# GpSimd makes three of eight query-key products, VectorE reads its queries from PSUM, and the orders around them are rewritten

## The chip, the cores and the metric

The kernel runs on one core of a Trainium2 chip. The metric is the device time of one execution in microseconds; lower is better. The kernel before takes 84.03 us, the median of three runs (83.32 to 84.17).

## The reference, cut to what matters

Two layers with residuals on x of 8 images, 128 channels, 16 x 16 positions, all in float32. The first is a dilated 3 x 3 neighbourhood attention whose four channel groups of 32 (two heads of 16 each) have dilations 1, 2, 4 and 8; each group's output is scaled by a gate, a softmax over pooled features. The second is a channel attention with projections. Each layer normalises its input over groups of four channels.

```python
def L0(x, w_qkv, w_gate, b_gate):            # x is group-normalised
    qkv = einsum('bchw,oc->bohw', x, w_qkv).reshape(B, 3, 4, 32, H, W)
    for i, dil in enumerate((1, 2, 4, 8)):
        q, k, v = qkv[:, 0, i], qkv[:, 1, i], qkv[:, 2, i]
        # per head, per position: 9 neighbours at distance dil, zero outside
        attn = softmax(einsum('bhdn,bhdkn->bhnk', q, unfold3x3(k)) * 16 ** -0.5)
        outs[i] = einsum('bhnk,bhdkn->bnhd', attn, unfold3x3(v))
    gate = softmax(x.mean(axis=(2, 3)) @ w_gate.T + b_gate)
    return concatenate([outs[i] * gate[:, i] for i in range(4)])

def L1(x, W, b, W_proj, b_proj):             # x is group-normalised
    p = (einsum('oc,bchw->bohw', W, x) + b).reshape(B, 4, 32, 256)
    att = softmax(einsum('bhdn,bhen->bhde', p, p) * 256 ** -0.5)
    return einsum('oc,bchw->bohw', W_proj, einsum('bhde,bhen->bhdn', att, p)) + b_proj

x = x + L0(gn(x));  x = x + L1(gn(x))
```

## The kernel before

Every engine has an order written out by hand, and semaphores tie the orders together. The first layer works in two phases `ph` (even and odd images), and within a phase in four units `s`, one for each dilation; a unit (ph, s) holds 32 channels of four images on 128 partitions. The stages are:

- **Loads.** SyncE and ScalarE issue the loads of x in six pieces (`load_x`). SyncE loads the matrix that averages over a channel group (`C_GRP` of `cs`) between the first and the second of its pieces.
- **First norm.** VectorE sums, ScalarE sums squares, TensorE averages over groups (`first_stats`, L817), VectorE makes the variance (`norm_variance`, L536), GpSimd the power -0.5 (`rsqrt`, L334), then VectorE and ScalarE normalise. TensorE runs dummy matmuls between (`keep_clock`, L812) on the first slot of `xt`.
- **Projections.** `project` (L828) makes a tile of queries, keys or values in PSUM and ScalarE copies it out (`copy_tile`, L405), 21 tiles in five banks. Three units' queries, (0,0), (1,2) and (1,3), stay in PSUM (`project_query`, L847).
- **Products.** VectorE multiplies queries by shifted keys (`multiply_qk`, L582), three chunks a unit. TensorE sums them over channels of a head into scores (`sum_scores`, L864).
- **Softmax.** VectorE shifts (`softmax_shift`), ScalarE takes the exponential, VectorE divides (`softmax_divide`, L611) and multiplies in the gate, which GpSimd works out from L354 on. The result is `prob`.
- **Values.** TensorE spreads `prob` over channels (`spread`, L890), three chunks a unit, in two PSUM places by turns; VectorE multiplies by shifted values (`multiply_pv`, L621); the nine neighbours are added, eight additions a unit, by GpSimd for units (0,0) to (0,3), (1,0) and (1,1) (L374), and by VectorE for (1,2) (`add_neighbours`, L641). For (1,3) TensorE adds them up itself (`sum_second`, L924).
- **Back to images.** `restore(0)` and `restore(1)` (L911) put phase 0 back into image layout after GpSimd's 32nd addition; `sum_second` does so for phase 1. VectorE adds the residual (`first_residual`), ScalarE squares, TensorE averages (`group_stats`), VectorE makes the variance (`second_variance`), GpSimd the power (placed among its additions by `RSQRT_AFTER`), VectorE the bias (`second_norm_bias`, `nbias`), and ScalarE normalises (`norm`, L435).
- **Second layer**, in four groups of two images: projection, transposes, channel attention, softmax, fused projection, last residual, stores. TensorE's order has `attention(1)` of the second group just ahead of `sum_second`, so phase 1 of the first layer isn't put back before phase 0's attention is made.

Of the kernel before, what the change touches and what calls it, by code (L numbers as in the profile page):

```python
# [31 lines left out]
ARRIVAL = (0, 2, 6, 4, 1, 3, 5, 7)  # L32
NORMS_ON_DVE = ((2, 0), (3, 0), (3, 1))
# [7 lines left out]
RSQRT_AFTER = ((1, 0, 4), (1, 1, 0))  # L41
# [10 lines left out]
C_ID, C_GRP, C_RED, C_DIL, C_END = 0, 128, 256, 384, 388  # L52
# [52 lines left out]
def build(nc, x, wpack, consts, selc, out):  # L105
    with ExitStack() as ctx:
# [6 lines left out]
        xt = sb("xt", [P, B, N])  # L113
# [25 lines left out]
        warm = sb("warm", [P, 1])  # L139

# [31 lines left out]
        PROJ_BANKS = (0, 1, 2, 3, 6)  # L172
        IDLE_BANK = 5
        BANK = (4, 6, 0, 2)
        Q_IN_PSUM = [(0, 0, 0)] + [(0, s, PHASES - 1) for s in range(2, ND)]

        def q_columns(s):

            return 512 * SC[0] + N * (s % 2) if s else 512 * IDLE_BANK
# [6 lines left out]
        grp_loaded = sem("grp_loaded")  # L186
# [4 lines left out]
        cells_set = sem("cells_set")  # L191
        sum_ready = sem("sum_ready")
# [16 lines left out]
        qk_ready = sem("qk_ready")  # L209
        scores_ready = sem("scores_ready")  # L210
# [38 lines left out]
        tiles = []  # L249
        for ph in range(PHASES):  # L250
            tiles += [(kind, s, ph) for s in range(ND) for kind in (0, 1) if (kind, s, ph) not in Q_IN_PSUM]
            tiles += [(2, s, ph) for s in range(ND)]

        def x_slice(i):

            piece = X_PIECES[i]
            return slice(piece[0], piece[-1] + 1, PHASES)
# [26 lines left out]
        def _(sp):  # L284
            xv = x.rearrange("b c n -> c b n")

            def load_x(i):

                bs = x_slice(i)
                sp.dma_start(xt[:, bs, :], xv[:, bs, :]).then_inc(x_loaded[i], 16)  # L290
# [21 lines left out]
        def _(pool):  # L312
# [31 lines left out]

            pool.wait_ge(nbias_ready, PHASES)
# [16 lines left out]
            nc.gpsimd.tensor_tensor(gate[:], gsel[:], grec[:], ALU.mult).then_inc(gate_ready, 1)  # L362

# [19 lines left out]
        def _(act):  # L383
            xv = x.rearrange("b c n -> c b n")
            for i in (1, 3):
                bs = x_slice(i)
                act.dma_start(xt[:, bs, :], xv[:, bs, :]).then_inc(x_loaded[i], 16)
# [4 lines left out]
            def square_sum(n):  # L392
# [3 lines left out]
                nc.scalar.activation(xn1[:, b // GB, b % GB, :], xt[:, b, :], ACT.Square,  # L396
                                     accum_out=sums[:, b, 1:2]).then_inc(square_ready, 1)

            def first_norm(b):

                act.wait_ge(nbias_ready, b % PHASES + 1)
                nc.scalar.activation(xn[:, b, :], xt[:, b, :], ACT.Identity, bias=nbias[:, b:b + 1],
                                     scale=rstd[:, b:b + 1]).then_inc(xn_act_ready, 1)

            def copy_tile(n):  # L405
# [4 lines left out]
                act.wait_ge(proj_ready, n + 1)  # L410
                src = ps[:, PROJ_BANKS[n % len(PROJ_BANKS)], 0:N]
# [56 lines left out]
            for n in range(1, 3):  # L468
# [3 lines left out]
            copy_tile(3)  # L472
            copy_tile(4)
            copy_tile(5)
            first_norm(5)
            first_norm(7)
            for n in range(6, 12):
                copy_tile(n)
            gate_exp()
            for n in range(12, 17):  # L480
                copy_tile(n)
            softmax_exp(0)
            for n in range(17, len(tiles)):
                copy_tile(n)
            softmax_exp(1)
            squares(0)
# [33 lines left out]
        def _(dve):  # L520
# [7 lines left out]

            link(nc.vector.memset(signs[:, 0:1], -1.0))
# [31 lines left out]
            def channel_sum(n):  # L561
# [3 lines left out]
                nc.vector.tensor_reduce(sums[:, b, 0:1], xt[:, b, :], AX.X, ALU.add).then_inc(sum_ready, 1)  # L565

            def first_norm(b):
                dve.wait_ge(rstd_ready, b % PHASES + 1)
                nc.vector.tensor_scalar(xn[:, b, :], xt[:, b, :], gst[:, b, 0:1], rstd[:, b:b + 1],
# [12 lines left out]
            def multiply_qk(ph, s, ci):  # L582

                if ci == 0:
                    dve.wait_ge(proj_copied, tiles.index((1, s, ph)) + 1)
# [556 lines left out]
```

## Time and profile before

| | |
|---|---|
| median of three runs | 84.03 us (83.32 to 84.17) |
| the profiled execution | 84.19 us, of which the span of the trace is 82.3 us |
| TensorE matmul busy | 69.5 us (84%) |
| VectorE busy | 67.4 us (82%) |
| GpSimd busy | 41.5 us (50%) |
| ScalarE busy | 29.4 us (36%) |

All later times are counted from the start of the span. In the rows PE is TensorE, DVE VectorE, ACT ScalarE, POOL GpSimd, SP SyncE. A row of the timeline merges neighbouring instructions of one kind; a float32 matmul leaves two records, so x24 is 12 matmuls. A number in square brackets at a row's end is how long the engine sat idle before it, with the one that released it.

### The profile page before, as it was taken

Reading aid. Unit: us, or ns where it says so; the run is one execution under the profiler, and the core shown is the slowest. Engines: PE = TensorE matmul, PEld = TensorE weight load, DVE = VectorE, ACT = ScalarE, POOL = GpSimd, SP = SyncE. Lnnn points to the kernel's source line nnn. Section 1 sums busy time; section 2 is a strip of 40 time slices with the busy share of each in tenths; the row PEclk is TensorE's granted clock in tenths of the full one; section 3 lists DMA queues with packets and bytes.
Section 4 is the critical chain, followed back from the end, with each engine's and each line's share of the span. In section 5 each row is a group of like instructions: output and inputs, shape, how many; then the busy total and the mean of one; then the engine's idle time right before and its main releaser. Section 6 shows DMA issues by size and latency. Waiting matters only on the chain.

```text
span 82.3 us, 2430 instructions
## 1 busy us (share of the span) xinstructions
PE 69.5 (84%) x988; PEld 49.5 (60%) x988; DVE 67.4 (82%) x183; ACT 29.4 (36%) x92; POOL 41.5 (50%) x84
## 2 busy tenths in 40 slices
PE   0379999699995699899978879679999999999960
PEld 0369876266752359566768654368677768566530
DVE  1242869999999998999999699889999998587860
ACT  1852652992377000000020001240795362765210
POOL 7104105850770007999999999699992004200000
PEclk9999999999999999999999999999999999999999
DMA  0973046000000000000000000000000000002253
GB/s 4 284 223 127 0 92 158 15 0 0 8 0 4 0 4 8 0 0 0 4 8 0 0 0 0 0 0 8 0 0 0 8 0 8 4 33 94 79 176 127
DMA packets 3195, 3.04 MB, mean 37 GB/s; under 512 B 368, under 2 KB 3056, under 8 KB 3184
## 3 DMA queue, kind: packets, MB, share of 16 engines
q1 hardware_dynamic: 2896, 2.63, 11.5%
q10 hardware_dynamic: 288, 0.26, 0.9%
q8 instruction: 7, 0.11, 0.6%
q14 instruction: 4, 0.03, 0.1%
HBM read 1.84 MB, written 1.05 MB: 35 GB/s over the span
## 4 chain that ended last, share of the span: by engine, by line
DVE 50%; PE 28%; POOL 6%; issue 5%; DMA 5%; ACT 2%; SPq 1%; DVEq 0%
PE ps L810 26%; DVE qk L597 18%; DVE pv L638 12%; DMA xt<-x_dram 5%; POOL acc L374 3%; DVE acc L650 2%; DVE pv L650 2%; DVE x L669 2%; DVE prob L617 2%; DVE smax L604 2%; POOL rstd L337 2%; DVE ssum L614 2%; POOL pv L374 2%; DVE acc L638 1%; PE ps L967 1%
## 5 line engine op out<-in xcount | busy, mean ns | idle before, releaser
L810 PE MATMUL ps<-prob,sel 64*128 64x192 f32 (+6 forms) x192 | 17.8, 313 | 2.7 <-DVE pv L638 1.6
L810 PE MATMUL ps<-xn,wp 128*32 128x256 f32 (+1 forms) x208 | 18.0, 409 | 0.8 <-ACT q L413 0.7
L638 DVE TENSOR_TENSOR pv<-ps,v 128x128 f32<-128x128 f32 (+7 forms) x32 | 17.1, 567 | 1.8 <-PE ps L810 0.8
L810 PEld LDWEIGHTS ps<-prob,sel 64*128 64x128 f32 x192 | 13.6, 186 | 6.9 <-DVE pv L638 3.5
L810 PE MATMUL ps<-xt 128*128 128x128 f32 x60 | 11.7, 337 | 3.5 <-DMA xt<-x_dram 3.5
L374 POOL TENSOR_TENSOR pv<-pv 128x240 f32<-128x240 f32 (+3 forms) x24 | 14.1, 599 | 0.5 <-DVE pv L638 0.5
L337 POOL TENSOR_TENSOR rstd<-gvar,mhalf 128x2 f32<-128x2 f32 (+1 forms) x6 | 4.9, 809 | 17.0 <-DVE gvar L544 17.0
L810 PEld LDWEIGHTS ps<-xn,wp 128*32 128x32 f32 (+1 forms) x208 | 9.7, 122 | 5.9 <-ACT xn L439 1.3
L374 POOL TENSOR_TENSOR acc<-acc,pv 128x256 f32<-128x256 f32 (+4 forms) x20 | 12.7, 638 | 0.5
L810 PEld LDWEIGHTS ps<-xt 128*128 128x128 f32 x60 | 9.6, 232 | 4.8 <-DMA xt<-x_dram 3.5
L597 DVE TENSOR_TENSOR qk<-q,k 128x672 f32<-128x672 f32 (+7 forms) x21 | 11.4, 606 | 0.0
L810 PE MATMUL ps<-qk,cs 128*32 128x192 f32 (+6 forms) x176 | 7.7, 302 | 0.8 <-ACT v L416 0.8
L424 ACT ACTIVATE ps<-shifted 128x576 f32<-128x576 f32 x2 | 1.3, 655 | 16.7 <-DVE shifted L607 16.7
L597 DVE TENSOR_TENSOR qk<-ps,k 128x128 f32<-128x128 f32 (+6 forms) x15 | 6.4, 482 | 0.8 <-PE ps L810 0.8
L810 PEld LDWEIGHTS ps<-qk,cs 128*32 128x32 f32 x176 | 4.8, 109 | 3.5 <-ACT v L416 1.3
L432 ACT ACTIVATE pT<-x 128x256 f32<-128x256 f32 x8 | 3.3, 409 | 10.1 <-DVE x L669 10.1
L374 POOL TENSOR_TENSOR acc<-pv 128x256 f32<-128x256 f32 x4 | 2.9, 728 | 6.3 <-DVE pv L638 6.3
L565 DVE TENSOR_REDUCE sums<-xt 128x1 f32<-128x256 f32 x8 | 2.9, 413 | 3.1 <-DMA xt<-x_dram 3.1
L810 PE MATMUL ps<-p,mT 128*128 128x256 f32 x16 | 4.9, 410 | 0.3 <-ACT mT L459 0.3
L701 DVE SCALAR_TENSOR_TENSOR x<-ps,wp,x 128x256 f32<-128x256 f32 x8 | 3.7, 479 | 0.7 <-PE ps L810 0.7
L396 ACT ACTIVATE xn<-xt 128x256 f32<-128x256 f32 x8 | 3.3, 408 | 2.2 <-DMA xt<-x_dram 2.2
L439 ACT ACTIVATE xn<-x,nbias,rstd 128x256 f32<-128x256 f32 x5 | 2.7, 591 | 3.5 <-DVE nbias L550 3.5
(81 smaller groups left out, 89.6 us busy)
## 6 DMA issues: line engine op xcount, KB each, us to landing
out_dram<-x SPq DMA_DIRECT2D x8, 128.0 KB, 1.7
xt<-x_dram SPq DMA_DIRECT2D x2, 256.0 KB, 4.6
xt<-x_dram ACTq DMA_DIRECT2D x2, 128.0 KB, 2.9
xt<-x_dram SPq DMA_DIRECT2D x2, 128.0 KB, 3.2
sel<-selc_dram SPq DMA_DIRECT2D x4, 64.0 KB, 2.1
wp<-wpack_dram SPq DMA_DIRECT2D x1, 194.0 KB, 4.3
wp<-wpack_dram SPq DMA_DIRECT2D x1, 131.0 KB, 2.7
cs<-consts_dram SPq DMA_DIRECT2D x2, 64.0 KB, 2.6
```

The costliest lines, as they stand in the source:

```text
L337: nc.gpsimd.tensor_tensor(rstd[:, bs], gvar[:, bs], mhalf[:, bs], ALU.pow).then_inc(rstd_ready, 1)
L374: nc.gpsimd.tensor_tensor(o, a, b, ALU.add).then_inc(added, 1)
L396: nc.scalar.activation(xn1[:, b // GB, b % GB, :], xt[:, b, :], ACT.Square, accum_out=sums[:, b, 1:2]).then_inc(square_ready, 1)
L432: nc.scalar.activation(pT[:, g, 2 * i:2 * i + 2, :].rearrange("p t n -> p (t n)"), x1[:, b, :], ACT.Square, accum_out=sums1[:, b, 1:2]).th ...
L439: nc.scalar.activation(xn1[:, g, i, :], x1[:, b, :], ACT.Identity, bias=nbias[:, b:b + 1], scale=rstd[:, b:b + 1]).then_inc(xn1_act_ready, 1)
L565: nc.vector.tensor_reduce(sums[:, b, 0:1], xt[:, b, :], AX.X, ALU.add).then_inc(sum_ready, 1)
L597: last = nc.vector.tensor_tensor(o, a, b, ALU.mult)
L604: link(nc.vector.tensor_reduce(smax[:], view(ps, 512 * SC[ph], [[1, QP], [256, 3], [QP, 3]]), AX.XY, ALU.max))
L638: last = nc.vector.tensor_tensor(o, a, b, ALU.mult)
L650: nc.vector.tensor_tensor(o, a, b, ALU.add).then_inc(dve_added, 1)
L701: nc.vector.scalar_tensor_tensor(out=x1[:, b, :], in0=ps[:, BANK[g] + i, 0:N], scalar=wp[:, W_BP:W_BP + 1], in1=x1[:, b, :], op0=ALU.add, ...
L810: return nc.tensor.matmul(o, w, m, start=start, stop=stop)
```

## The change

- GpSimd makes the products of units (0,3), (1,2) and (1,3) (`multiply_qk` of its own, both operands in SBUF). The first two stand ahead of the gate's arithmetic, the third between the gate and the additions.
- VectorE makes the other five, all with the queries in PSUM (`Q_AT`); the order of its units in phase 0 is now 0, 2, 1.
- 19 tiles are copied by ScalarE instead of 21, from three banks, the six last value tiles later from halves of banks 4 and 5.
- `first_stats(1)` moves behind `project(2)`; it stood behind `project(1)`.
- The dummy matmuls read a tile `idle` that VectorE sets first of all; seven of them start without waiting for x. Four did so after x's first slot.
- The group matrix stands ahead of x's first slot in DRAM and comes in its rows; one load fewer. x is laid out in the order of its pieces.
- Around the second norm: VectorE does `add_neighbours(1, 2)` ahead of both `second_norm_bias`; `restore(0)` and what follows stand later among the chunks; GpSimd's two powers come after the eighth addition of (1,0) and the third of (1,1).

```diff
-RSQRT_AFTER = ((1, 0, 4), (1, 1, 0))
+RSQRT_AFTER = ((1, 0, 7), (1, 1, 2))
...
-        PROJ_BANKS = (0, 1, 2, 3, 6)
+        PROJ_BANKS = (0, 1, 6)
+        VALUE_BANKS = (4, 5)
...
+        Q_AT = {(0, 0): 512 * 5, (0, 2): 512 * 3, (0, 1): 512 * 2, (1, 0): 512 * 3, (1, 1): 512 * 2}
+        DVE_PRODUCTS = list(Q_AT)
+        POOL_PRODUCTS = [(0, 3), (1, 2), (1, 3)]
+        SUM_ORDER = [(0, 0), (0, 2), (0, 1), (0, 3), (1, 0), (1, 2), (1, 1), (1, 3)]
...
             load_x(0)
-            sp.dma_start(cs[:, C_GRP:C_GRP + P], consts[:, C_GRP:C_GRP + P]).then_inc(grp_loaded, 16)
             load_x(2)
...
+            def multiply_qk(ph, s):
+
+                pool.wait_ge(proj_copied, max(copied_by(0, s, ph), copied_by(1, s, ph)))
+                if ph:
+                    pool.wait_ge(scores_ready, summed(0, s))
+                for ci in range(3):
+                    for o, a, b in query_operands(ph, s, ci):
+                        last = nc.gpsimd.tensor_tensor(o, a, b, ALU.mult)
+                last.then_inc(pool_qk_ready, 1)
+
...
+            multiply_qk(0, 3)
+            multiply_qk(1, 2)
 
             pool.wait_ge(gexp_ready, 1)
...
             nc.gpsimd.tensor_tensor(gate[:], gsel[:], grec[:], ALU.mult).then_inc(gate_ready, 1)
+            multiply_qk(1, 3)
...
+            nc.vector.memset(idle[:], 1.0).then_inc(idle_set, 1)
...
-            pe.wait_ge(x_loaded[0], 16)
-            keep_clock(4)
+            pe.wait_ge(idle_set, 1)
+            keep_clock(7)
             first_stats(0)
             keep_clock(5)
+            pe.wait_ge(w_loaded, 16)
+            wait_norms(0)
             project(0)
             project_query(0, 0)
-            project(1)
+            for n in range(1, 3):
+                project(n)
             first_stats(1)
```

The second norm on VectorE. Before, the variance of group 1 is followed by two chunks of `multiply_pv`, both biases, and the rest; the eight additions (acc and pv out of pv) come later:

```order
L541 TENSOR_TENSOR gst<-ps,signs 128x2x2
L543 TENSOR_TENSOR gsq<-gst 128x2
L544 SCALAR_TENSOR_TENSOR gvar<-gst,gsq 128x2
L638 TENSOR_TENSOR acc<-ps,v 128x256
L638 TENSOR_TENSOR pv<-ps,v 128x2x192
L638 TENSOR_TENSOR pv<-ps,v 128x16x12
L638 TENSOR_TENSOR pv<-ps,v 128x2x12x12
L550 TENSOR_TENSOR nbias<-gst,rstd 128x2 x2
L638 TENSOR_TENSOR pv<-ps,v 128x16x12
L638 TENSOR_TENSOR pv<-ps,v 128x2x12x12
```

In the changed kernel, from the same variance on:

```order
L586 TENSOR_TENSOR gst<-ps,signs 128x2x2
L588 TENSOR_TENSOR gsq<-gst 128x2
L589 SCALAR_TENSOR_TENSOR gvar<-gst,gsq 128x2
L688 TENSOR_TENSOR acc<-acc,pv 128x192
L688 TENSOR_TENSOR pv<-pv 128x12x12
L688 TENSOR_TENSOR acc<-acc,pv 128x192
L688 TENSOR_TENSOR pv<-pv 128x12x12 x2
L688 TENSOR_TENSOR acc<-acc,pv 128x16x12
L688 TENSOR_TENSOR pv<-pv 128x12x12
L688 TENSOR_TENSOR acc<-acc,pv 128x16x12
L595 TENSOR_TENSOR nbias<-gst,rstd 128x2 x2
L676 TENSOR_TENSOR pv<-ps,v 128x16x8
```

All of unit (1,2) and the first chunk of (1,3) have moved ahead of the variance, and the eight additions stand between it and the biases.

TensorE at the same place, from `group_stats(1)` (ps<-sums) on; ps<-prob,sel is `spread`, ps<-xt `keep_clock`, ps<-xn,wp the second projection, L967 the transposes, ps<-pT the attention, ps<-acc the start of `sum_second`. Before:

```order
L810 MATMUL ps<-prob,sel 128x2x4x12
L810 MATMUL ps<-xt 128x128
L810 MATMUL ps<-prob,sel 128x2x4x16 x4
L810 MATMUL ps<-xn,wp 128x256 x4
L967 MATMUL ps<-cs,p 128x128 x4
L810 MATMUL ps<-prob,sel 128x2x4x8 x8
L967 MATMUL ps<-cs,p 128x128 x2
L810 MATMUL ps<-pT 32x32 x16
L967 MATMUL ps<-cs,p 128x128 x2
L810 MATMUL ps<-pT 32x32 x16
L810 MATMUL ps<-acc,cs 32x256 x16
```

In the changed kernel (ps<-idle is `keep_clock`):

```order
L834 MATMUL ps<-sums,gx 128x4
L834 MATMUL ps<-idle 128x128 x2
L834 MATMUL ps<-prob,sel 128x2x4x8 x4
L834 MATMUL ps<-xn,wp 128x256 x4
L834 MATMUL ps<-prob,sel 128x2x4x8 x4
L1000 MATMUL ps<-cs,p 128x128 x6
L834 MATMUL ps<-pT 32x32 x16
L1000 MATMUL ps<-cs,p 128x128 x2
L834 MATMUL ps<-pT 32x32 x16
L834 MATMUL ps<-acc,cs 32x256 x16
```

Between the group average and the second projection there are now two dummies and one chunk of `spread`; before, four chunks and three dummies stood there. One chunk instead of two stands ahead of the transposes that remain.

GpSimd around the gate. Before:

```order
L351 COPY pexp<-pooled 128x128 x2
L356 TENSOR_TENSOR gpick<-gex,cs 128x8
L357 TENSOR_TENSOR gtwo<-gex 128x4
L358 TENSOR_TENSOR gsum<-gtwo 128x2
L359 TENSOR_TENSOR grec<-gsum,minus 128x2
L360 TENSOR_TENSOR gpick<-gpick 128x2x2
L361 TENSOR_TENSOR gsel<-gpick 128x2
L362 TENSOR_TENSOR gate<-gsel,grec 128x2
L374 TENSOR_TENSOR acc<-pv 128x256
```

In the changed kernel, from the last two of the twelve products ahead of the gate to the first of the six behind it:

```order
L384 TENSOR_TENSOR qk<-q,k 128x16x12
L384 TENSOR_TENSOR qk<-q,k 128x2x12x12
L400 TENSOR_TENSOR gpick<-gex,cs 128x8
L401 TENSOR_TENSOR gtwo<-gex 128x4
L402 TENSOR_TENSOR gsum<-gtwo 128x2
L403 TENSOR_TENSOR grec<-gsum,minus 128x2
L404 TENSOR_TENSOR gpick<-gpick 128x2x2
L405 TENSOR_TENSOR gsel<-gpick 128x2
L406 TENSOR_TENSOR gate<-gsel,grec 128x2
L384 TENSOR_TENSOR qk<-q,k 128x16x8
```

The gate now waits for two units of products on its own engine, and the additions for a third.

## Rows read from the trace of the kernel before

**Rows 1.** The page: busy time by engine, and the ended-last chain's shares.

```profile
PE 69.5 (84%) x988; PEld 49.5 (60%) x988; DVE 67.4 (82%) x183; ACT 29.4 (36%) x92; POOL 41.5 (50%) x84
...
DVE 50%; PE 28%; POOL 6%; issue 5%; DMA 5%; ACT 2%; SPq 1%; DVEq 0%
```

**Rows 2.** Chain that ended last: start, length, what; head and sum_second's end.

```profile
1.64 3.76 DMA xt<-x_dram
...
66.16 1.46 DVE x L669 x8
```

**Rows 3.** Timeline of TensorE: start, length, instructions; head and second projection to sum_second.

```profile
3.48 2.08 PE L810 MATMUL ps<-xt 128*128 128x128 f32 x8 [3.48 <-DMA xt<-x_dram]
...
9.01 3.01 PE L810 MATMUL ps<-xn,wp 128*32 128x256 f32 x24
...
12.27 2.80 PE L810 MATMUL ps<-xn,wp 128*32 128x256 f32 x48
...
58.74 2.17 PE L810 MATMUL ps<-xn,wp 128*128 128x256 f32 x8
...
64.31 0.73 PE L810 MATMUL ps<-acc,cs 32*32 32x256 f32 x32
```

**Rows 4.** Timeline of VectorE: products of units (1,2) and (1,3).

```profile
31.86 0.71 DVE L597 TENSOR_TENSOR qk<-ps,k 128x192 f32<-128x192 f32 x2
...
33.54 1.51 DVE L597 TENSOR_TENSOR qk<-ps,k 128x256 f32<-128x256 f32 x4
...
36.59 1.53 DVE L597 TENSOR_TENSOR qk<-ps,k 128x128 f32<-128x128 f32 x6
```

**Rows 5.** GpSimd by shape: count, busy us, mean ns of one.

```profile
L374 POOL TENSOR_TENSOR acc<-pv 128x256 f32<-128x256 f32 x4 | 2.9, 728 | 6.3 <-DVE pv L638 6.3
...
L337 POOL TENSOR_TENSOR rstd<-gvar,mhalf 128x2 f32<-128x2 f32 x4 | 2.8, 705 | 7.6 <-DVE gvar L544 7.6
...
L374 POOL TENSOR_TENSOR pv<-pv 128x64 f32<-128x64 f32 x4 | 1.2, 311 | 0.0
```

**Rows 6.** Timeline of GpSimd: pooled features, gate, first and last additions.

```profile
14.42 0.21 POOL L346 TENSOR_TENSOR pooled<-sums,per_n 128x8 f32<-128x8 f32 x1
14.71 0.77 POOL L347 TENSOR_TENSOR pooled<-pooled,rstd 128x8 f32<-128x8 f32 x1
...
16.41 1.16 POOL L351 COPY pexp<-pooled 128x128 f32<-128x128 f32 x2
...
32.02 0.70 POOL L374 TENSOR_TENSOR pv<-pv 128x240 f32<-128x240 f32 x1 [0.52 <-DVE pv L638]
...
49.08 0.73 POOL L374 TENSOR_TENSOR acc<-pv 128x256 f32<-128x256 f32 x1
...
61.52 0.68 POOL L374 TENSOR_TENSOR acc<-acc,pv 128x224 f32<-128x224 f32 x1
```

**Rows 7.** Timeline of VectorE: softmax 0's end, and around the second norm.

```profile
27.38 0.82 DVE L617 SCALAR_TENSOR_TENSOR prob<-ps,gate,srec 128x576 f32<-128x576 f32 x1
...
55.51 0.55 DVE L544 SCALAR_TENSOR_TENSOR gvar<-gst,gsq 128x2 f32<-128x2 f32 x1
55.98 0.41 DVE L638 TENSOR_TENSOR acc<-ps,v 128x256 f32<-128x256 f32 x1
...
57.41 0.65 DVE L550 TENSOR_TENSOR nbias<-gst,rstd 128x2 f32<-128x2 f32 x1
...
58.81 0.42 DVE L638 TENSOR_TENSOR acc<-ps,v 128x256 f32<-128x256 f32 x1
...
59.48 0.73 DVE L650 TENSOR_TENSOR acc<-acc,pv 128x192 f32<-128x192 f32 x1
...
61.58 1.00 DVE L650 TENSOR_TENSOR pv<-pv 128x144 f32<-128x144 f32 x2
62.51 0.34 DVE L650 TENSOR_TENSOR acc<-acc,pv 128x192 f32<-128x192 f32 x1
```

**Rows 8.** Timeline of ScalarE: the second norm of phase 0.

```profile
58.09 2.08 ACT L439 ACTIVATE xn<-x,nbias,rstd 128x256 f32<-128x256 f32 x4 [3.52 <-DVE nbias L550]
```

More of the change, by code:

```diff
@@ L467, in _ @@
             square_sum(7)
-            for n in range(1, 3):
+            for n in range(1, 4):
                 copy_tile(n)
@@ L886, in sum_scores @@
                         m = view(qk[s], (3 * ci + i0) * N + QP * j + c0, dims(3 * N, N))
[L887 removed]
+                        last = mm(o, w, m, start=(s == 0), stop=(final and ci > 0))
                 last.then_inc(scores_ready, 1)
@@ L1010, in _ @@
+            project_query(0, 2)
+            project(4)
+            project_query(0, 1)
+            sum_scores(0, 0)
+            project(5)
+            gate_logits()
+            sum_scores(0, 2)
+            wait_norms(1)
+            for n in range(6, 9):
                 project(n)
-            sum_scores(0, 0)
-            for n in range(9, 11):
+            project_query(1, 0)
+            sum_scores(0, 1)
+            sum_scores(0, 3)
+            for n in range(9, 12):
                 project(n)
-            sum_scores(0, 1)
@@ L1031, in _ @@
-            sum_scores(1, 1)
-            keep_clock(1)
-            spread(0, 1, 2)
-            spread(0, 2, 0)
-            sum_scores(1, 2)
-            keep_clock(1)
-            for i in range(1, 3):
-                spread(0, 2, i)
-            sum_scores(1, 3)
-            for i in range(2):
+            project_query(1, 1)
+            sum_scores(1, 0)
+            project(12)
+            sum_scores(1, 2)
+            spread(0, 0, 0)
+            for n in range(EARLY, EARLY + 2):
+                project(n)
@@ new lines, in _ @@
+            spread(0, 0, 1)
+            spread(0, 0, 2)
+            spread(0, 1, 0)
+            sum_scores(1, 1)
+            spread(0, 1, 1)
+            sum_scores(1, 3)
+            spread(0, 1, 2)
+            for n in range(EARLY + 2, EARLY + 4):
+                project(n)
+            spread(0, 2, 0)
+            for n in range(EARLY + 4, EARLY + 6):
+                project(n)
+            spread(0, 2, 1)
+            pe.wait_ge(proj_copied, EARLY + 4)
+            keep_clock(2)
+            spread(0, 2, 2)
@@ L1041, in _ @@
+            for i in range(3):
                 spread(0, 3, i)
             keep_clock(2)
-            spread(0, 3, 2)
-            keep_clock(6)
-            for i in range(3):
-                spread(1, 0, i)
-            spread(1, 1, 0)
+            for s in range(2):
+                for i in range(3):
+                    spread(1, s, i)
+            spread(1, 2, 0)
             restore(0)
-            spread(1, 1, 1)
+            spread(1, 2, 1)
+            restore(1)
+            spread(1, 2, 2)
@@ L1063, in _ @@
                 project_second(1, i)
+            spread(1, 3, 2)
             for i in range(2):
                 transpose(0, i)
-            for i in range(1, 3):
-                spread(1, 3, i)
             transpose(1, 0)
```

243 lines of the change are left out of this document (116 added, 127 removed).

## The prediction

> **What bounds the kernel now.** The page comes first: TensorE is busy 84% and VectorE 82% of the span, GpSimd 50%, and the chain that ended last is 50% VectorE and 28% TensorE [rows 1]. So neither of the two is the bound alone; the chain has to be read by stretches.
>
> In the head, the load of the fourth slot of x takes 3.76 us of the chain, to 5.40 [rows 2]. TensorE then makes the first projections slowly: 12 matmuls in 3.01 us, 0.25 us each, and 24 in 2.80 us, 0.12 us each, from 12.27 on [rows 3]. The page's clock line shows full grant throughout; the records show the lower of the two levels (1.2 and not 2.4 GHz) for the first twelve. TensorE had been idle up to 3.48 and on dummies from then on.
>
> From 12 to 57 us VectorE hardly rests, and GpSimd's additions run without a break from 32.02 to 49.08 (phase 0) and on to 62.20 [rows 6]. TensorE follows the two.
>
> The stretch that decides is the second norm of phase 0. Its variance ends at 56.06, its first bias at 58.06 [rows 7], ScalarE's norms start at 58.09 [rows 8], TensorE's second projection at 58.74, and `sum_second` at 64.31, directly behind `attention(1)` in TensorE's order [rows 3]. VectorE's last residuals of phase 1 end at 67.62 [rows 2]. What VectorE still does between 58 and 64.7 (additions, last chunks) lies beside that chain of 6.2 us (58.09 to 64.31). So at the end of the first layer the date that counts is that of the first bias, not that of VectorE's last chunk. All that is behind is the same in both kernels.
>
> **The change, part by part.**
>
> *Products off VectorE.* Unit (1,2) costs it 0.71 + 1.51 = 2.2 us, (1,3) 1.53, and (0,3) has the shapes of (1,3): 5.25 us less work [rows 4]. Reading a query in PSUM costs what reading it in SBUF does (the rows of (1,2) and (1,3) are themselves from PSUM, and run beside GpSimd's additions without stretching), so the two added PSUM units are costed at nothing.
>
> *Products on GpSimd.* An addition of 256 columns takes 0.728 us, of 64 columns 0.311 [rows 5]; that is 0.17 us and 2.17 ns a column. Multiplications of this size there are none; an addition reads and writes as much, and I take its price. (0,3) and (1,3) are two instructions of 256 and four of 128 columns each: 1.46 + 4 x 0.45 = 3.25, less the 0.03 us by which neighbours overlap, 3.1 us. (1,2) is 256, 384 and twice 192 and 288 columns: 4.4 us. The gate's inputs come some 1.1 us sooner, since an operation on eight columns took 0.77 us beside VectorE's products of two SBUF operands, one just like it before them 0.21, and two of them stood so [rows 6]: `pexp` ends at 16.4 and not 17.57. Then (0,3) to 19.5, (1,2) to 23.9, the gate's seven small operations, at 0.29 us from start to start (14.42 to 14.71) and 0.4 more for the power (0.705 on two columns) [rows 5, 6], 2.4 us, to 26.3, (1,3) to 29.4. VectorE, with 1.5 us of (0,3) gone from its own path, wants the gate at about 25.9 and had `prob` at 27.38 [rows 7]. So softmax 0 comes about 1.1 us sooner and is held by the gate for 0.3. The additions then start behind the first two value chunks, at 30.7 and not 32.02; they run as densely as before, so the 32nd ends at 47.8 and not 49.08, and all 48 at 60 and not 62.20. From softmax 0 on GpSimd has no gap in which to catch up.
>
> *Head.* One load fewer ahead of the fourth slot: issued 0.5 us sooner, bounds 0 and 0.7 (then ScalarE's squares set the end). The clock: the early dummies start at about 1.05 and not 3.48. If TensorE stays at the lower level as before, `first_stats(1)` now has 16 matmuls ahead of it instead of 12, at 0.25 us, and that eats the 0.5 us; I take 0.2 gained. If it is at the upper level by the first projection, the variance of phase 1 comes 1.2 us sooner. Bounds 0 and 1.2. The row it is nearest to: before, the level was still low some 7 us after the first dummy, though they nearly filled that time; I take the lower gain.
>
> *VectorE up to the variance of group 1.* Before, it ended at 56.06. Off: 5.25 of products and 0.2 of the head. On: all of unit (1,2)'s values and the first chunk of (1,3)'s now stand ahead of it, 1.43 (55.98 to 57.41) + 0.7 + 0.67 (58.81 to 59.48) = 2.8 us [rows 7]. Six projections, a `sum_scores` and a wait for GpSimd's (1,3) now stand between the chunks of `spread` after softmax 0, and VectorE waits for them: 0.5 us more idle, by laying 0.8 to 1.0 us pieces of TensorE beside it. 56.06 - 5.25 - 0.2 + 2.8 + 0.5 = 53.9.
>
> *The eight additions ahead of the bias.* This is the term that turns the sum. Beside GpSimd's additions VectorE's own go at 0.70 us each (59.48 to 61.58, three of them); after GpSimd's end at 62.20 one takes 0.34 (at 62.51) [rows 6, 7]. GpSimd is now busy up to 60, so all eight go slowly: 5.6 us, to 59.5. The first bias itself takes 0.65 us in such company [rows 7]: 60.15. Before it was 58.06, so the norms start 2.1 us later. Bounds: eight at 0.34 (2.7 us, which brings the bias to 57.2) and eight at 0.70.
>
> *From the norms to `sum_second`.* ScalarE's four norms at 0.5 us go as before [rows 8]; one chunk of `spread` instead of two stands ahead of the last transposes, 0.45 us less. 6.2 becomes 5.75. `sum_second` starts at 65.9 instead of 64.31.
>
> *TensorE's idle time.* Behind `group_stats(1)` it has two dummies (0.5 us) and one chunk, done at about 53.7, then nothing until the norms at 60.2: 6.5 us idle. No stretch of before has such a gap after the start, so its price isn't shown. Bounds: nothing, and the chain of projections, transposes, attention and `sum_second` at the head's 0.25 for 0.12 until it rises again, some 3 us. The Trainium skill speaks against the change here: "TensorE: Matmul & The Clock Gate", section on the HAM clock gate, has the idle array fall back to 1.2 GHz and return only after sustained work. By the page the 3 us would come on top; I keep it as a rival and cost the forecast at nothing, for the one row at hand (the head) shows a low level after idling, not a fall.
>
> *Sum.* Profiled execution 84.19 + 2.1 - 0.45 = 85.85. The median lies 0.16 below it, so **85.7 us**, 2% slower.
>
> **Rivals.**
>
> *The clock falls in the new gap* (as above). For it: 6.5 us of idle, and the lower level after the idle head. Against: no fall in any row, and the dummies before the gap. 87 to 88.5, middle 87.8.
>
> *Early dummies raise the clock in time.* For it: seven dummies of 0.5 us fill 1.05 to 4.5. Against: a pause of nearly 1 us behind them, and before, some 7 us of dummies and projections hadn't been enough. All dates 1.0 us sooner: 84.7, no change that can be told.
>
> *The other side: VectorE's additions aren't slowed.* If they go at 0.34 us, as after 62.20, the bias comes 2.9 us sooner than forecast and the kernel takes 82.8. For it: the reordering halves what is left for GpSimd when VectorE comes to them, if GpSimd's multiplications are quicker than additions. Against: GpSimd would have to be done by 55, and its additions alone last until 60. It turns to faster once the eight cost under 3.1 us, which takes 2.5 off the forecast, or the variance comes before 51.4.
>
> *GpSimd's products cost more.* The gate stands behind two of them. Each 10% on their price is 0.75 us on softmax 0 and 1 us on the additions' start. At 1.3 times the price: 88.
>
> **How the numbers follow.** Forecast 0.40 (85.1 to 86.5 alone), clock falls 0.23, slow products 0.06, early clock 0.13, additions not slowed (or VectorE earlier than laid out) 0.18. Faster by over 1% is the last, 0.18; within 1% (83.2 to 84.9, about what a measurement of this kernel can tell from no change) the early clock and a little of the forecast, 0.18; slower 0.64. The range from 82.9 to 88.2 leaves out the extremes of the first and the last.
>
> **What would show it.** The steps, in the changed trace: TensorE's projections of phase 0 at 0.25 us each; GpSimd's `pexp` end at 16.4, gate end at 26.3, 32nd addition at 47.8, 48th at 60; `prob` at 26.3; variance of group 1 at 53.9; eight additions at 0.7 us; first bias at 60.2; a gap of about 6 us on TensorE ahead of the second projection, with records after it as long as at 58.74 (0.5 us each) if the clock held, and twice that if not; `sum_second` at 65.9. I would be wrong if the variance came before 51.4, if the additions went at 0.34 us, or if the first bias weren't what the tail hangs from.

## The result and the profile after

The changed kernel takes 89.7 us, the median of four runs (89.52 to 89.87), beside 84.07 for the kernel before on the same chip. The ratio is 1.072, with a 95% interval of 1.066 to 1.079. The direction was forecast and the size was not: 85.7 was expected, and 89.7 lies above the range's end of 88.2. In this and all later ratios only those runs of a kernel count that lie within 1.5% of its fastest, while the medians are over all its runs. The profiled execution took 89.82 us, with a span of 87.8.

The page of the changed kernel: busy time by engine, the clock line (tenths of full speed in 40 slices of 2.2 us), and the chain's shares.

```profile
PE 70.0 (80%) x974; PEld 50.0 (57%) x974; DVE 63.7 (72%) x166; ACT 29.2 (33%) x90; POOL 49.1 (56%) x102
...
PEclk9999579999999999999759999995558999999998
...
PE 45%; DVE 38%; issue 5%; ACT 4%; DMA 3%; POOL 1%; DVEq 0%; POOLq 0%
```

VectorE is busy for 3.7 us less and is down to 72%; 5.25 us of products had been laid out to go. GpSimd has 7.6 us more: 10.5 us of products, less some 3 us by which the small operations around its gate are shorter than before. But the chain, which had been half VectorE's [rows 1], is now first of all TensorE's, and the clock line has three dips that it didn't have before: near 9, near 43 and from 60 to 66 us. The stretches in numbers (start:end, TensorE's busy time and instructions, granted clock, DMA share, GB/s):

```profile
8.00:8.50 0.50, 0.00 (x0) 1.00 0.00 0
...
9.00:11.50 2.50, 2.50 (x27) 0.50 0.33 63
...
43.00:46.00 3.00, 3.00 (x20) 0.50 0.00 0
...
60.00:66.50 6.50, 3.70 (x8) 0.50 0.00 0
```

0.50 is the lower level, 1.2 and not 2.4 GHz. TensorE's timeline at the three places (start, length, instructions, in brackets the idle time before and its releaser):

```profile
5.76 1.36 PE L834 MATMUL ps<-idle 128*128 128x128 f32 x10
8.92 3.39 PE L834 MATMUL ps<-xn,wp 128*32 128x256 f32 x32 [1.79 <-DVE xn L614]
...
39.68 1.34 PE L834 MATMUL ps<-prob,sel 64*128 64x96 f32 x16 [0.73 <-DVE pv L676]
41.24 1.37 PE L834 MATMUL ps<-prob,sel 64*128 64x64 f32 x16 [0.22 <-DVE pv L676]
42.54 1.16 PE L834 MATMUL ps<-idle 128*128 128x128 f32 x4
43.62 5.50 PE L834 MATMUL ps<-prob,sel 64*128 64x192 f32 x40
...
62.80 3.78 PE L834 MATMUL ps<-xn,wp 128*128 128x256 f32 x8 [6.09 <-ACT xn L483]
...
69.81 0.73 PE L834 MATMUL ps<-acc,cs 32*32 32x256 f32 x32
```

Five dummies, ten instructions, in 1.36 us are nearly all at the upper level, at 0.14 us each (the 14 instructions from 1.05 on had taken 3.36, 0.24 each): TensorE had come to the upper level behind the early dummies. Then it was idle for 1.79 us. The granted clock is 1.00 up to 8.5 us, within this pause, and 0.50 behind it, and the first projections ran at the lower level. The second projection starts after 6.09 us of idling, and its eight instructions take 3.78 us where they took 2.17 [rows 3].

VectorE from the end of unit (1,2)'s values to the second norm:

```profile
56.15 0.15 DVE L586 TENSOR_TENSOR gst<-ps,signs 128x4 f32<-128x4 f32 x1
56.33 0.69 DVE L588 TENSOR_TENSOR gsq<-gst 128x2 f32<-128x2 f32 x1
57.06 0.59 DVE L589 SCALAR_TENSOR_TENSOR gvar<-gst,gsq 128x2 f32<-128x2 f32 x1
57.58 0.35 DVE L688 TENSOR_TENSOR acc<-acc,pv 128x192 f32<-128x192 f32 x1
57.84 0.82 DVE L688 TENSOR_TENSOR pv<-pv 128x144 f32<-128x144 f32 x1
...
60.85 0.71 DVE L688 TENSOR_TENSOR acc<-acc,pv 128x192 f32<-128x192 f32 x1
61.49 0.70 DVE L595 TENSOR_TENSOR nbias<-gst,rstd 128x2 f32<-128x2 f32 x2
```

The variance of group 1 ends at 57.65 and not at 53.9; the eight additions, 57.58 to 61.56, take 3.98 us and not 5.6; the norms start at 62.15 and not at 60.2.

GpSimd did what the sum said: three units of products, the gate between them.

```profile
16.00 3.08 POOL L384 TENSOR_TENSOR qk<-q,k 128x128 f32<-128x128 f32 x6
19.53 4.35 POOL L384 TENSOR_TENSOR qk<-q,k 128x192 f32<-128x192 f32 x6 [0.44 <-ACT q L457]
...
25.87 0.19 POOL L406 TENSOR_TENSOR gate<-gsel,grec 128x2 f32<-128x2 f32 x1
26.02 3.07 POOL L384 TENSOR_TENSOR qk<-q,k 128x128 f32<-128x128 f32 x6
```

### The profile page after: what moved, and what is told of

It reads as the page before. It is cut to its first block, busy times and chain, and to the rows that moved or that the text cites. A ratio compares the mean times of both kernels' runs of the same rounds, so it can differ in the third digit from the quotient of the medians.

```text
span 87.8 us, 2405 instructions
## 1 busy us (share of the span) xinstructions
PE 70.0 (80%) x974; PEld 50.0 (57%) x974; DVE 63.7 (72%) x166; ACT 29.2 (33%) x90; POOL 49.1 (56%) x102
## 3 DMA queue, kind: packets, MB, share of 16 engines
HBM read 1.84 MB, written 1.05 MB: 33 GB/s over the span
## 4 chain that ended last, share of the span: by engine, by line
PE 45%; DVE 38%; issue 5%; ACT 4%; DMA 3%; POOL 1%; DVEq 0%; POOLq 0%
PE ps L834 43%; DVE qk L635 10%; DVE pv L676 8%; DMA gx<-x_dram 3%; PE ps L1000 3%; DVE acc L688 2%; DVE pv L688 2%; ACT xn L440 2%; DVE x L707 2%; DVE ssum L652 2%; DVE smax L642 2%; DVE acc L676 1%; DVE gsq L588 1%; DVE srec L653 1%; DVE xn L614 1%
## 5 line engine op out<-in xcount | busy, mean ns | idle before, releaser
L834 PE MATMUL ps<-xn,wp 128*32 128x256 f32 (+1 forms) x208 | 20.5, 426 | 7.9 <-ACT xn L483 6.1
L834 PE MATMUL ps<-prob,sel 64*128 64x192 f32 (+6 forms) x192 | 19.7, 332 | 3.4 <-DVE prob L655 1.7
L635 DVE TENSOR_TENSOR qk<-ps,k 128x720 f32<-128x720 f32 (+6 forms) x18 | 12.2, 739 | 0.9 <-PE ps L834 0.9
L384 POOL TENSOR_TENSOR qk<-q,k 128x128 f32<-128x128 f32 (+4 forms) x18 | 10.5, 619 | 0.4 <-ACT q L457 0.4
L834 PE MATMUL ps<-idle 128*128 128x128 f32 x46 | 9.0, 346 | 1.1 <-DVE idle L573 1.1
L834 PEld LDWEIGHTS ps<-idle 128*128 128x128 f32 x46 | 7.7, 243 | 1.5 <-DVE idle L573 1.1
L460 ACT COPY k<-ps 128x256 f32<-128x256 f32 x8 | 3.0, 370 | 5.0 <-PE ps L834 4.8
L610 DVE TENSOR_REDUCE sums<-gx 128x1 f32<-128x256 f32 x8 | 2.9, 412 | 2.3 <-DMA gx<-x_dram 2.3
L489 ACT ACTIVATE p<-ps,wp 128x256 f32<-128x256 f32 x8 | 3.8, 472 | 1.5 <-PE ps L834 1.5
L460 ACT COPY v<-ps 128x256 f32<-128x256 f32 x8 | 2.7, 370 | 4.5 <-PE ps L834 4.5
(82 smaller groups left out, 85.5 us busy)
```

The costliest lines, as they stand in the source:

```text
L384: last = nc.gpsimd.tensor_tensor(o, a, b, ALU.mult)
L460: nc.scalar.copy(dst, src.rearrange("p (r c) -> p r c", c=W)).then_inc(proj_copied, 1)
L489: nc.scalar.activation(p1[:, g, i, :], ps[:, BANK[g] + i, 0:N], ACT.Identity, bias=wp[:, W_B1:W_B1 + 1]).then_inc(p1_copied, 1)
L610: nc.vector.tensor_reduce(sums[:, b, 0:1], xt(b), AX.X, ALU.add).then_inc(sum_ready, 1)
L635: last = nc.vector.tensor_tensor(o, a, b, ALU.mult)
L834: return nc.tensor.matmul(o, w, m, start=start, stop=stop)
```

## The experiments

Theory: the order is what costs. Both biases of the second norm stand behind eight additions of VectorE, and the second norm is what the end hangs from. Besides, three falls of TensorE's clock add a cost that the forecast had left out. Rival A: the clock is nearly all of it. Rival B: the products on GpSimd cost the time, through the gate or by slowing VectorE.

### The clock, each fall by itself

Five more dummies behind the first statistics:

```diff
 first_stats(0)
-keep_clock(5)
+keep_clock(10)
```

> The changed kernel (89.7 us) with ten dummy matmuls instead of five behind first_stats(0), so that TensorE isn't idle from 7.12 to 8.92. Theory A (the granted clock falls behind idle stretches and each fall costs by itself): the clock stays full at 8.5 to 11.9, the 16 matmuls ahead of first_stats(1) take 2 us and not 3.4, the variance of phase 1 comes 1.2 us sooner, and about 1 us of it reaches the end: 88.6. Theory B (TensorE isn't what the chain hangs from there, VectorE and GpSimd are): the clock may stay up but the time does not change, 89.7. Theory C (the fall has nothing to do with the idle stretch): the clock still reads 0.5 at 9 to 11.

It took 88.02 us (ratio to before 1.052, 1.042 to 1.062), 1.7 less than the change. The first projections run at the upper level now, but start 1.1 us later than in the change: the 20 instructions of the ten dummies, most of them at the lower level, lasted until 10.04. The statistics of phase 1 were read at 12.33 and not 12.67, so the head gave only 0.3 us. The profiled execution is 1.9 us shorter than the change's mostly because the clock didn't fall near 43 us in it, although nothing was changed there: VectorE waited 3.3 us and not 4.4 for the chunks. The gain can't be put down to the five dummies alone.

```profile
5.91 4.21 PE L834 MATMUL ps<-idle 128*128 128x128 f32 x20
10.04 1.94 PE L834 MATMUL ps<-xn,wp 128*32 128x256 f32 x32
```

The middle, with a dummy beside each of the small chunks:

```diff
-keep_clock(2)
+keep_clock(4)
 spread(0, 2, 2)
+keep_clock(1)
 for i in range(3):
     spread(0, 3, i)
+    keep_clock(1)
 keep_clock(2)
```

> The changed kernel with six more dummies between the chunks of units (0,2) and (0,3), at 38 to 43 us, where TensorE had pauses and the granted clock fell at 42.7 for 3.4 us. Theory A: the clock stays full, VectorE's wait of 2.2 us at 43 goes, restore(0) starts at 48.2 instead of 50.9, the variance of group 1 at about 55.1 instead of 57.7: 87.2. Theory B (GpSimd's additions, the 32nd at 47.9, hold the stretch): 89.0 or more.

90.14 us (three runs at 90.1 to 90.3, one at 88.69, that is 1.0 less than the change; the times leave open whether anything is won, and no ratio is given). The profiled execution, one of the three, shows no gain in the stretch that was edited. The granted clock is 1.00 from 40 to 46, and yet the way from the first `prob` to the variance of group 1 takes 31.3 us (26.51 to 57.83), and in the change 31.45 (26.20 to 57.65): VectorE's waits between 27 and 57 are 2.7 + 1.3 + 0.4 = 4.4 us, as much as with the fall. The dummies stand ahead of the chunks that VectorE waits for, which is the likely reason.

The gap ahead of the second projection, filled:

```diff
 spread(1, 3, 1)
+keep_clock(20, BANK[1] + 1)
 for i in range(2):
     project_second(0, i)
```

> The changed kernel with twenty dummies (5.4 us) ahead of the second projection, in the 6.1 us in which TensorE waited for ScalarE's norms. Theory A: no fall at 59.7, the way from the norms' start to sum_second is 5.8 us instead of 7.7: 87.8. Theory B (ScalarE's norms and copies set that way): 89.5.

87.4 us (1.037, 1.026 to 1.048), 2.3 less than the change.

```profile
55.90 4.73 PE L834 MATMUL ps<-idle 128*128 128x128 f32 x40
62.09 2.17 PE L834 MATMUL ps<-xn,wp 128*128 128x256 f32 x8 [1.45 <-ACT xn L483]
...
67.50 0.73 PE L834 MATMUL ps<-acc,cs 32*32 32x256 f32 x32
```

From the second projection to `sum_second` it is 5.41 us instead of 7.01: the fall at the end costs 1.6. The rest of the 2.3 lies ahead of the norms. In this execution the clock didn't fall there although nothing was changed in it, and VectorE waited 3.3 us and not 4.4 (the head was 0.5 us later, which takes part of it back).

All three together:

> All three additions of dummies together. Theory A: the granted clock is 1.0 throughout and the time is 84.5 to 85.5, near the forecast of 85.7 that was made without falls of the clock; what is left above before is the first bias, late behind the eight additions. Theory B: over 88. If the falls only move to other places, 86 to 88 with a mean clock under 0.97.

87.29 us (1.038, 1.028 to 1.049), no better than the last one alone, with a granted clock of 1.00 throughout. If the clock were nearly all, 84.5 to 85.5 had been expected. Rival A falls: with no fall left, the kernel is still 3.8% slower than before. Without its falls the change would lose some 2.4 of its 5.6 us; since the dummies cost something too, this is the net of both.

### The order

The change with the biases ahead of the additions, nothing else:

```diff
 second_variance(1)
-add_neighbours(1, 2)
 second_norm_bias(0)
 second_norm_bias(1)
+add_neighbours(1, 2)
```

> The changed kernel with one edit: both second_norm_bias ahead of add_neighbours(1, 2) on VectorE, as before the change. Order theory (the bias behind the eight additions is the main cost, first by itself and then through the idle stretch it gives TensorE): the norms start at about 58.5 instead of 62.15, TensorE waits 2 us and not 6.1 for them, no fall of the clock at 59.7, sum_second at about 65 because VectorE's last column now comes then: 85.0 to 85.5. Upstream theory (the loss is made before the variance: chunks that wait for TensorE, the fall at 42.7): the gain is under 2 us, 88.

85.66 us (1.029, 1.019 to 1.039), 4.0 less. The clock was low at both ends as in the change (0.53 from 7 to 14 us, 0.54 from 58 to 65.5), although no fall had been expected at the second projection. In the middle it didn't fall in this profiled execution (1.00 from 42 to 47), and the variance of group 1 ends at 56.88, 0.8 us sooner than in the change, for reasons that aren't the edit's.

```profile
56.80 0.15 DVE L595 TENSOR_TENSOR nbias<-gst,rstd 128x2 f32<-128x2 f32 x1
58.24 0.63 DVE L595 TENSOR_TENSOR nbias<-gst,rstd 128x2 f32<-128x2 f32 x1 [1.29 <-POOL rstd L369]
```

The first bias comes at 56.80 instead of 61.49, and `sum_second` at 66.09 instead of 69.81. The second bias now waits 1.29 us for GpSimd, whose power for group 1 stands behind three of its additions. The next run gives a comparison without the difference in the middle.

The same with the five dummies of the head:

> The same with ten dummies instead of five behind first_stats(0). Order theory and clock theory together: another 1.0 to 1.5 us off, 84.0, about the time of the kernel before. Upstream theory: 87.

84.95 us (84.2 to 87.12; ratio 1.012, 1.000 to 1.025). Beside the change with the same ten dummies (88.02) the profiled executions are alike up to the variance of group 1, which ends at 55.98 here and at 56.08 there, without a fall in the middle in either. `sum_second` starts at 64.00 instead of 67.88: 3.9 us are the order's, with what it does to the clock behind it.

The kernel before with the order of the change:

```diff
-second_norm_bias(0)
-second_norm_bias(1)
 multiply_pv(1, 2, 2)
 multiply_pv(1, 3, 0)
 add_neighbours(1, 2)
+second_norm_bias(0)
+second_norm_bias(1)
```

> The kernel before (84.0) with the changed kernel's order: both second_norm_bias behind multiply_pv(1,2,2), (1,3,0) and add_neighbours(1, 2). Order theory: the first bias at about 62 instead of 57.4, minus what VectorE saves behind it; TensorE idle for 4 us or more ahead of the second projection, with a fall of the granted clock there: 88 to 90. Upstream theory: under 86.

91.69 us, beside 83.58 (1.101, 1.093 to 1.110), above the 88 to 90 that order theory had given. So the order alone, without one product on GpSimd, costs the kernel before 8.1 us. The eight additions take 3.9 us in it, and TensorE idles 5.50 us and falls to the lower level:

```profile
63.17 3.78 PE L810 MATMUL ps<-xn,wp 128*128 128x256 f32 x8 [5.50 <-ACT xn L439]
...
70.66 0.73 PE L810 MATMUL ps<-acc,cs 32*32 32x256 f32 x32
```

And the same with 18 dummies ahead of the second projection:

> The same with eighteen dummies in TensorE's wait ahead of the second projection. It tells the two costs of the order apart: the late bias alone should leave 87 to 88 with a granted clock of 1.0, and the fall should be the 1.5 to 2.5 us between this run and the one without dummies. If the fall costs nothing there, the two are the same.

89.18 us (1.072, 1.062 to 1.082); the granted clock is 1.00, the eight take 2.17 again. By the medians, 5.6 of the 8.1 us are the late bias (3 to 4 had been expected) and 2.5 the fall that comes with it; from the norms' start to `sum_second` the two profiled executions differ by 2.0 (8.14 and 6.17).

### GpSimd's additions beside VectorE

The change with all its dummies (87.29), in which GpSimd's additions but the first of each unit work on one element a partition. It leaves out most of GpSimd's share of the sums, and keeps the instructions and their order:

```diff
 o, a, b = operands(ph, s, n, target, slot)
+if n:
+    o, a, b = (t[:, 0:1, 0:1] for t in (o, a, b))
 nc.gpsimd.tensor_tensor(o, a, b, ALU.add).then_inc(added, 1)
```

> The changed kernel with all dummies (head, middle, gap; 87.3 us), in which GpSimd's additions but the first of each unit work on one element a partition: most of its share of the sums is left out, the instructions and their order stay. If GpSimd's additions are what slows VectorE's small operations and additions: gsq and gvar of group 1 at 0.16 instead of 0.70 and 0.60, the eight additions in 2.5 us instead of 3.8, and the first bias 2.4 us sooner, so about 85. If VectorE's lost time in the middle (4.4 us of waits for TensorE's chunks between 27 and 57) is the exchange between the two, these waits stay and the variance of group 1 moves by no more than 1 us. Rival: GpSimd's additions hold up VectorE by the waits for its buffers: then the waits go too and the variance comes 2 us sooner or more.

85.84 us (1.028, 1.019 to 1.036). VectorE's second norm in it:

```profile
55.99 0.69 DVE L590 TENSOR_TENSOR gsq<-gst 128x2 f32<-128x2 f32 x1
56.72 0.16 DVE L591 SCALAR_TENSOR_TENSOR gvar<-gst,gsq 128x2 f32<-128x2 f32 x1
56.79 0.36 DVE L690 TENSOR_TENSOR acc<-acc,pv 128x192 f32<-128x192 f32 x1
57.08 0.30 DVE L690 TENSOR_TENSOR pv<-pv 128x144 f32<-128x144 f32 x1
...
58.88 0.22 DVE L597 TENSOR_TENSOR nbias<-gst,rstd 128x2 f32<-128x2 f32 x2
```

and GpSimd at the same time:

```profile
55.94 0.72 POOL L421 TENSOR_TENSOR acc<-pv 128x256 f32<-128x256 f32 x1
56.62 0.19 POOL L421 TENSOR_TENSOR pv<-pv 128x1 f32<-128x1 f32 x1
```

The eight additions go in 2.1 us instead of 3.9, `gvar` in 0.16 instead of 0.60. `gsq`, for which 0.16 had been expected, still takes 0.69, and it lies beside the one addition of GpSimd that has its full width, 55.94 to 56.66: its record ends at 56.68, right behind that one's. This is what the Trainium skill says in "SBUF — State Buffer", section on the two separate sides: an operation of VectorE with two SBUF inputs and one of GpSimd lock each other out for a whole instruction, whoever comes first. The trace agrees, and with the other half of it too: GpSimd's products at 16.00 and 26.02 take the 3.1 us of the addition's price beside VectorE's products, which have one operand in PSUM.

VectorE's waits between 27 and 57 us, before, in the change, and here (total us, times, longest):

```profile
DVE pv L638 <- PE ps L810: 0.8, 3, 0.3
DVE pv L638 <- issue: 0.7, 1, 0.7
DVE gst L541 <- PE ps L810: 0.2, 1, 0.2
```

```profile
DVE pv L676 <- issue: 2.2, 1, 2.2
DVE pv L676 <- PE ps L834: 2.2, 7, 0.7
```

```profile
DVE pv L678 <- PE ps L836: 2.7, 8, 0.7
DVE pv L678 <- issue: 1.3, 1, 1.3
DVE acc L678 <- PE ps L836: 0.4, 1, 0.4
```

1.7, 4.4 and again 4.4 us. The run with all dummies and GpSimd's additions at full width has the same three rows as this one, and from the first `prob` to the variance of group 1 it takes 31.3 us against 30.9 here. So these waits aren't made by GpSimd's additions: they lie between TensorE's chunks and VectorE's products of them. Before, unit products of 0.7 to 1.5 us stood between the chunks and, as these rows are read here, gave TensorE its time [rows 4]; no run put such work back, so this cause is argued and not shown.

Of rival B the gate falls by the change's own trace: the first `prob` starts at 26.20, 1.2 us sooner than before. Against the products as the main cause stands the kernel before, which loses 8.1 us by the order without one of them on GpSimd. A run with the three products back on VectorE in the new order wasn't made. The lock is a real cost, but one that the kernel before paid too (its eight additions took from 59.48 to 63.38).

### The early dummies in the kernel before

```diff
-pe.wait_ge(x_loaded[0], 16)
-keep_clock(4)
+pe.wait_ge(idle_set, 1)
+keep_clock(7)
 first_stats(0)
-keep_clock(5)
+keep_clock(10)
```

(with the tile of ones and its semaphore, as the change has them)

> The kernel before with the early dummies alone: seven on a tile of ones at the start, ten instead of five behind the first statistics, all loads as before. If the lower level in the head is what cost the kernel before its slow projections: 24 matmuls at 9.01 take 1.6 us instead of 3.0, the variance of phase 1 comes 1.2 us sooner and the kernel takes 82.9. Rival: the head waits for x and the sums in any case, and what is won at 12 is lost in waits for ScalarE's copies and the gate: 83.5 to 84.

84.29 us beside 83.41 (1.009, 1.002 to 1.016), no gain and a little above the 83.5 to 84 of the rival, which was right.

```profile
5.93 4.38 PE L813 MATMUL ps<-idle 128*128 128x128 f32 x20
10.24 1.50 PE L813 MATMUL ps<-xn,wp 128*32 128x256 f32 x24
```

24 matmuls take 1.50 us instead of 3.01 [rows 3], but they start 1.2 us later, behind dummies at the lower level. The statistics of phase 1 are read at 12.32 instead of 12.41, and from there to `sum_second` both take 51.9 us.

### A version with the gain of the change and without its loss

Biases ahead of the additions, one chunk of products in VectorE's wait between them, GpSimd's power for group 1 one addition earlier, ten dummies in the head, eight ahead of the second projection:

```diff
-RSQRT_AFTER = ((1, 0, 7), (1, 1, 2))
+RSQRT_AFTER = ((1, 0, 7), (1, 1, 1))
...
 second_variance(1)
-add_neighbours(1, 2)
 second_norm_bias(0)
+multiply_pv(1, 3, 1)
 second_norm_bias(1)
-for i in range(1, 3):
-    multiply_pv(1, 3, i)
+add_neighbours(1, 2)
+multiply_pv(1, 3, 2)
...
-keep_clock(5)
+keep_clock(10)
...
 spread(1, 3, 1)
+keep_clock(8, BANK[1] + 1)
```

> The changed kernel with the biases ahead of the eight additions and five more dummies in the head, as in the run before it of that kind (84.95), and three things more: the power for group 1 stands one GpSimd addition earlier, the second of unit (1,3)'s chunks stands between the two biases (VectorE waited 1.3 us there), and eight dummies stand ahead of the second projection. Order theory: the bias of group 1 comes about 0.6 us sooner, the chunk costs VectorE nothing, TensorE doesn't fall to 0.5 at the second projection (it stood there from 56.8 to 60.3): 83.2, 1% under the kernel before. Rival (the products on GpSimd save nothing, because the middle stretch is bound by TensorE and VectorE waiting for each other): no better than the kernel before, 84 or more.

82.99 us (81.61 to 83.38) beside 83.41: ratio 0.981, 0.972 to 0.989. The ratio rests on two of six runs, 81.61 and 81.67; the other four took 82.86 to 83.38, within what the kernel before takes (82.66 to 84.5), and the medians differ by 0.5% only. The profiled execution had one of the early heads: its statistics of phase 1 are read at 11.17. From there to `sum_second` it takes 50.4 us, and the kernel before 51.9. So the change is worth some 1.5 us behind the head once the second norm doesn't wait. How much of that is due to the products on GpSimd isn't separated from its other parts.

```profile
53.91 2.05 PE L834 MATMUL ps<-idle 128*128 128x128 f32 x16
55.80 1.08 PE L834 MATMUL ps<-xn,wp 128*128 128x256 f32 x4
57.12 1.19 PE L834 MATMUL ps<-xn,wp 128*128 128x256 f32 x4 [0.24 <-ACT xn L483]
...
61.54 0.73 PE L834 MATMUL ps<-acc,cs 32*32 32x256 f32 x32
```

The same without the eight dummies:

> The same without the eight dummies ahead of the second projection. If the fall there still costs: the granted clock falls to 0.5 during the projection and the time is 0.5 to 1 us more than with them (83.9). If the gap is too short now for a fall: the same time.

84.72 us (82.6 to 85.43; 0.999, 0.989 to 1.010).

```profile
55.68 3.61 PE L834 MATMUL ps<-xn,wp 128*128 128x256 f32 x8 [1.71 <-ACT xn L483]
```

Here an idle time of 1.71 us, from 53.97 on, was followed by a fall: the granted clock is 1.00 up to 55.5 and 0.50 from 56 to 59, and the eight take 3.61. The two profiled executions agree to 0.1 us up to there; `sum_second` starts 1.0 us later. The medians differ by 1.7, more than this one fall explains in the profile.

### The runs side by side, without the head

The head takes different times in different executions of the same code: the statistics of phase 1 lie 1.2 us apart in three traces of the kernel before, and 1.3 in six of the change's variants with ten dummies. The way from the statistics of phase 1 (VectorE's first `gst` of it) to `sum_second` leaves it out. It is read from one profiled execution each:

| kernel | statistics read at, us | from there to `sum_second`, us |
|---|---|---|
| before | 12.41 | 51.9 |
| before, early dummies | 12.32 | 51.9 |
| before, biases late | 11.37 | 59.3 |
| the same, gap filled | 12.61 | 57.3 |
| the change | 12.67 | 57.1 |
| head dummies | 12.33 | 55.6 |
| middle dummies | 12.97 | 57.1 |
| gap filled | 13.18 | 54.3 |
| all dummies | 11.21 | 55.4 |
| all dummies, thin additions | 12.45 | 53.5 |
| biases first | 13.13 | 53.0 |
| biases first, head dummies | 12.24 | 51.8 |
| the last version without its eight dummies | 11.16 | 51.4 |
| the last version | 11.17 | 50.4 |

The change loses 5.2 us here. With the gap filled and no fall in the middle it is 2.8 less, so the two later falls are about half of it; the dummies in the middle cost 1.1 of it again. With the biases first and head dummies nothing is left of the loss, one fall at the second projection included.

## Why the prediction was right in direction and wrong in size

*The order decides: right, but not by the size that was given.* The date of the first bias is what the end hangs from, and putting it behind eight additions costs more than the products bring. Taking that one step back gives 4.0 us, and the step alone makes the kernel before 8.1 us slower. Yet the direction of the forecast owes something to luck: with the additions at the 3.84 us that they took from the variance to the biases, and not 5.6, its own sum gives 84.05, no change. What made it come out slower all the same was a later variance than the sum had and a fall of the clock that it left out.

*GpSimd's products: right.* 3.08, 4.35 and 3.07 us against 3.1, 4.4 and 3.1; `pexp` ended at 16.05 (16.4 was given), the gate at 26.06 (26.3), and `prob` started at 26.20 (26.3). GpSimd's second addition started at 30.84 (30.7), the 32nd ended at 47.94 (47.8). The 48th ended at 62.84 and not at 60, since GpSimd waited 2.22 us for the variance of group 0, which came late with everything of VectorE's.

*The head: the load right, the gain wrong.* The fourth slot came sooner, and the statistics of phase 0 were read at 5.95 instead of 6.68, the upper one of the bounds. The early clock, a rival at 0.13, did come, but TensorE's next pause (5.76 + 1.36 = 7.12 to 8.92) threw it away, so that the statistics of phase 1 were read at 12.67 and not 0.2 sooner than 12.41. `prob` wasn't held by the gate: the gate ended at 26.06, VectorE's own `srec` at 26.16, and `prob` started 0.04 us behind that, as it did before. It came 13.5 us after the statistics of phase 1, as in all ten traces of the changed kernel and its variants. So 26.20 against the forecast's 26.3 is luck: a head 0.26 us later than before stands where a wait for the gate was laid out.

*The variance of group 1: mis-sized, 53.9 against 57.65.* This is the step that failed first. Four terms of it:

- Up to `prob` the sum took 1.7 us off: 1.5 of products and 0.2 of the head. The text itself had laid out only 1.1, for the gate. The trace gives 1.2, since the products brought 1.4 and the head cost 0.26: 0.5 us.
- VectorE's waits for TensorE's chunks were put at 0.5 us more; they rose by 2.7, from 1.7 to 4.4. So 2.2 us were missing. Of the rise, 1.1 is the fall of the clock at 43 (the waits are 3.3 us in all six traces without it and without dummies there), and 1.6 is what is left, which the rows suggest to be missing cover, though no run tests it. The working laid TensorE's pieces beside VectorE's one by one and left out that with short products on one side and the next chunk on the other, each waits for the other in turn.
- `gsq` and `gvar` of this group took 0.69 and 0.59, where before they had taken 0.16 and 0.55: 0.6 us of lock, a term that was missing.
- Some 0.5 us are left unassigned.

*Eight additions at 0.7 us: too dear by 1.6.* They took 3.98. The price was read from the first three [rows 7]; the whole of before's eight, up to 63.38, took 3.90. Some of them last 0.7 to 0.8 us beside an addition of GpSimd, and others start 0.27 us after the one before; with GpSimd's additions thin, all eight took 2.2 (56.79 to 58.97).

*The clock at the gap: a rival at 0.23, costed at nothing, and it came.* From the norms to `sum_second` it took 7.66 us and not 5.75. The filled gap shows 1.6 of these 1.9 to be the fall; the 3 us given as the bound were too much; the granted clock was back at 0.96 between 66.5 and 67. The Trainium skill ("TensorE: Matmul & The Clock Gate", section on the HAM clock gate) had said that it would fall, and by the rows it did: 0.50 from 60 to 66.5, in and behind 6.09 us of idling. That no row of before showed a fall after idling was no reason to price it at nothing: there was no such idle time in it.

In sum: 85.85, plus 3.75 for the variance, minus 1.8 for the additions (from 57.65 to the biases' start at 61.49 it is 3.84), plus 1.9 behind the norms, gives 89.7; the profiled execution took 89.82. So the steps that failed are two: the variance of group 1, 3.75 us late above all by VectorE's waits (2.7 us more and not 0.5), and the fall of the clock at the gap, put at nothing and measured at 1.6. The third error, the additions, hid 1.8 us of them. The rival for faster (additions not slowed) had its mechanism half right; with eight additions at 3.84 by the forecast's own sum it would have needed the variance before 54.0 to be faster at all.

## What to carry to other kernels

When work is moved off a busy engine, follow the one small instruction that the next stage waits for: here an order that puts a bias behind eight additions cost more than 5 us of saved products brought. Ask of each new pause of TensorE what the stage behind it costs at the lower clock, and put dummies only where TensorE is idle anyway: here they gave 1.6 us in the gap, and ahead of chunks that are waited for they cost as much as they saved. And look for what the removed work had covered: VectorE's waits for TensorE rose by 1.6 us, and with the fall of the clock by 2.7, where 5.25 us of work were taken away.

## What the runs showed of the hardware

- The granted clock can be wrong at the start. It is given as 1.00 up to 7 us in all fourteen traces, while the first 14 instructions of the early dummies took 3.22 to 3.36 us; at the upper level 20 of the same took 2.48. In the runs with middle dummies and with the gap filled it is 1.00 up to 14 us, while the first projections took 3.50 and 3.64 us, and 1.94 at the upper level. In the head go by the records' durations.
- When the level rises differs between executions of the same head by some 3 us. With ten dummies behind the first statistics, their 20 instructions took 2.48 us in three kernels (the upper level from 5.8 on) and 4.14 to 4.38 in four others (by their durations at the lower until about 9), and in the changed kernel's variants among them `prob` started between 24.7 and 26.0. The kernel before has it too: with the same head, the statistics of phase 1 were read at 12.41 in it and at 11.37 and 12.61 in two of its variants. The Trainium skill ("TensorE: Matmul & The Clock Gate", section on the HAM clock gate) names the same thing, that the number of slow matmuls at the start is not the same in each run. A profile's single execution is thus no measure of a head's gain here, and differences of about 1 us between kernels with different heads stay open for the same reason.
- Pauses of 1.79 us (head) and 1.71 us (second projection) were followed by the lower level; so was, in the change's trace and in no other, the stretch behind pauses of 0.73 and 0.22 us. What made the difference isn't shown.
